# Perceiver layer on one core: the gate-up product kept in PSUM instead of an SBUF tile

## The reference

```
mlp = jax.nn.silu(hidden_states @ Wg + bg) * (hidden_states @ Wu + bu) @ Wd + bd
return mlp + experts_states
```

## Time and profile before

| | |
|---|---|
| median of 3 runs | 934.58 us |
| the profiled execution: its time | 934.41 us |
| the profiled execution: its span | 932.6 us |
| mean granted TensorE clock | 0.969 of full |
| busy: PE, DVE, ACT, POOL | 860.3, 598.5, 467.6, 316.4 us |
| chain that ended last | PE 78%, DVE 11%, ACT 4%, issue 3%, POOL 2%, DMA 1% |

### The profile page before, as it was taken

The page is one execution under the profiler, slowest core; times in us unless marked ns, Lnnn a source line. Parts: engine busy times, 40 slices in busy tenths (PEclk is TensorE's granted clock), DMA queues, the critical chain, the costliest instruction groups (busy, mean ns, idle before and its releaser), DMA issues.

```text
span 932.6 us, 17101 instructions
## 1 busy us (share of the span) xinstructions
PE 860.3 (92%) x6297; PEld 804.8 (86%) x6297; DVE 598.5 (64%) x1542; ACT 467.6 (50%) x1033; POOL 316.4 (34%) x290
## 2 busy tenths in 40 slices
PE   3699999999999999999999999999778777978997
PEld 2599999999999999999999999998567767877885
DVE  6445556556577877555656666776685386765885
ACT  3455554654556564545455555565343254633552
POOL 3544521302021313131220200221692477743442
PEclk9899999999999999999999999999988798989999
DMA  6175332232323232223223233423361042222320
GB/s 195 47 252 159 123 120 91 91 95 91 115 91 129 101 133 92 89 71 123 91 91 118 70 135 113 142 97 100 99 212 60 1 147 91 91 91 81 101 91 24
DMA packets 45219, 99.13 MB, mean 106 GB/s; under 512 B 3744, under 2 KB 16976, under 8 KB 41936
## 3 DMA queue, kind: packets, MB, share of 16 engines
q1 hardware_dynamic: 45040, 98.00, 31.2%
q10 hardware_dynamic: 96, 0.02, 0.0%
HBM read 88.06 MB, written 8.91 MB: 104 GB/s over the span
## 4 chain that ended last, share of the span: by engine, by line
PE 78%; DVE 11%; ACT 4%; issue 3%; POOL 2%; DMA 1%; DVEq 0%; SPq 0%; ACTq 0%
PE pJ L1654 14%; PE pJ L1655 14%; PE pJ L1656 14%; PE pV L1793 7%; PE pS L1771 4%; PE pT L1779 3%; PE pS L1779 3%; PE pT L1771 2%; PE pS L1654 2%; POOL WS L624 2%; PE pS L1656 2%; PE pS L1655 2%; PE pX L1694 1%; DVE KV L1132 1%; DVE late L1611 1%
## 5 line engine op out<-in xcount | busy, mean ns | idle before, releaser
L1654 PE MATMUL pJ<-WV,XT 128*128 128x256 f32 x544 | 159.5, 293 | 0.0
L1655 PE MATMUL pJ<-WV,XT 128*128 128x256 f32 x544 | 154.7, 284 | 0.0
L1656 PE MATMUL pJ<-WV,XT 128*128 128x256 f32 x544 | 154.5, 284 | 0.0
L866 ACT ACTIVATE SP<-SP,xneg 128x768 f32<-128x768 f32 (+1 forms) x96 | 85.8, 895 | 115.4 <-DVE xneg L1239 115.4
L1654 PE MATMUL pJ<-XT,WK 128*128 128x384 f32 (+1 forms) x384 | 126.8, 330 | 4.3 <-POOL XT L657 2.6
L1656 PE MATMUL pJ<-XT,WK 128*128 128x384 f32 (+1 forms) x384 | 125.2, 326 | 0.0
L1655 PE MATMUL pJ<-XT,WK 128*128 128x384 f32 (+1 forms) x384 | 125.1, 326 | 0.0
L1132 DVE TENSOR_TENSOR KT<-pJ,KT 128x384 fp32r<-128x384 f32 x96 | 51.3, 535 | 98.0 <-ACT KT L843 97.9
L657 POOL TENSOR_TENSOR XT<-xtmp,XT 128x384 fp32r<-128x384 f32 (+1 forms) x44 | 41.3, 938 | 196.8 <-ACT XT L827 196.5
L1654 PEld LDWEIGHTS pJ<-WV,XT 128*128 128x128 f32 x544 | 105.1, 193 | 0.2 <-issue 0.2
L1655 PEld LDWEIGHTS pJ<-WV,XT 128*128 128x128 f32 x544 | 105.2, 193 | 0.0
(11 more groups left out here) (362 smaller groups left out, 2177.4 us busy)
## 6 DMA issues: line engine op xcount, KB each, us to landing
WV<-wv_split SPq DMA_DIRECT2D x20, 1024.0 KB, 5.8
WK<-wk_split SPq DMA_DIRECT2D x40, 512.0 KB, 3.6
xraw<-in_ctx SPq DMA_DIRECT2D x7, 768.0 KB, 4.7
wk_split<-WK SPq DMA_DIRECT2D x8, 512.0 KB, 3.7
wv_split<-WV SPq DMA_DIRECT2D x4, 1024.0 KB, 6.5
work<-in_L_ffn_Wd SPq DMA_DIRECT2D x4, 1024.0 KB, 5.2
raw<-in_L_ffn_down_embed SPq DMA_DIRECT2D x8, 512.0 KB, 5.1
work<-in_L_ffn_up_embed SPq DMA_DIRECT2D x4, 1024.0 KB, 5.5
```

The source lines that it names most:

```text
L866: ac.activation(SP[:, I % 2, h, 0:w], SP[:, I % 2, h, 0:w], ACT.Exp, bias=xneg[:, I % 2, h:h + 1], scale=XSC, accum_out=total).then_inc(c_ ...
L1654: te.matmul(dst, a(HI), b(HI), start=start, stop=False)
L1655: te.matmul(dst, a(HI), b(LO), start=False, stop=False)
L1656: return te.matmul(dst, a(LO), b(HI), start=False, stop=stop)
```

## The change

L1587 writes its result back to the PSUM columns from which it reads the up product, instead of to `MA`. L1066 and L1132 read it from there. The bank is thus in use until L1132 is done, so `gate_up` of the tile after next waits for `s_al` in place of `s_a`, and so does the expert transposition `turn(0)`, which writes the first of these banks after tile 15's gates. No instruction is added or removed.

```
@@ -1063,7 +1063,7 @@
                 if ft >= 2:
                     act.wait_ge(s_mo, ft - 1)
-                ac.activation(ACTT[:, ft % 2, HI, :], MA[:, ft % 2, :], ACT.Copy).then_inc(s_ah, 1)
+                ac.activation(ACTT[:, ft % 2, HI, :], pS[:, ft % 2, T2:2 * T2], ACT.Copy).then_inc(s_ah, 1)
@@ -1584,10 +1584,10 @@
                 link(ve.scalar_tensor_tensor(out=MS, in0=pS[:, ft % 2, 0:T2], scalar=1.0, in1=MG[:, ft % 2, :],
                                              op0=ALU.add, op1=ALU.mult))
-                ve.scalar_tensor_tensor(out=MA[:, ft % 2, :], in0=pS[:, ft % 2, T2:2 * T2], scalar=vec[:, Kbu + ft:Kbu + ft + 1],
+                ve.scalar_tensor_tensor(out=pS[:, ft % 2, T2:2 * T2], in0=pS[:, ft % 2, T2:2 * T2], scalar=vec[:, Kbu + ft:Kbu + ft + 1],
                                         in1=MS, op0=ALU.add, op1=ALU.mult).then_inc(s_a, 1)
                 dve.wait_ge(s_ah, ft + 1)
-                low(ACTT[:, ft % 2, LO, :], MA[:, ft % 2, :], ACTT[:, ft % 2, HI, :]).then_inc(s_al, 1)
+                low(ACTT[:, ft % 2, LO, :], pS[:, ft % 2, T2:2 * T2], ACTT[:, ft % 2, HI, :]).then_inc(s_al, 1)
@@ -2016,7 +2016,7 @@
                 if ft >= 2:
-                    pe.wait_ge(s_a, ft - 1)
+                    pe.wait_ge(s_al, ft - 1)
@@ -2062,7 +2062,7 @@
                 else:
-                    pe.wait_ge(s_a, 15)
+                    pe.wait_ge(s_al, 15)
                     turn(0)
```

## The result

The changed kernel takes 926.03 us (median of 4 runs, 925.19 to 926.82) against 934.77 for the kernel before. The ratio is 0.9908, 95% interval 0.989 to 0.9925: 8.7 us faster. That is the forecast direction, but 3 us more than the 5.8 forecast, and inside the range (926.0 to 931.8) by 0.03 us only. The profiled execution took 925.19 us; its span is 923.4, which is 9.2 shorter than before.

A forecast was written before the change was run, and what follows sets the result against it. DVE sets the time in the dense half's front, L1132 running one after the other with POOL. Tile gains sum to 5.5 us, L1066 adds 0.2: 934.4 - 5.7 = 928.7, given as 928.8; range 926.0 to 931.8.

The forecast's parts named there:

- L1132 at 0.42 us with one input in PSUM: DVE's low part in all 16 tiles: 0.42 us instead of 858 ns on average, busy time down 6.9 us.
- Tiles 1 to 3: Gain 1.4 us at tile 1, cut to 1.0 by ACT's queue, then 1.8, 2.8, and 3.7 at the 772.08 matmul.
- POOL's two pieces, tiles 5 and 6: Two of eight POOL pieces PE waits for lose an L1132: 2 x 0.2 = 0.4 us, sum 4.1.
- Tiles 10 and 11: L1561 taken as waiting behind POOL, sum 4.3 us; L1132 of tile 11 adds 0.9, sum 5.2.
- L1587 in PSUM at no cost: L1587 writing to PSUM: 0 us taken, from a span of -0.2 to +2.4 on five of the path's tiles.
- the rival on the slower side: L1587's write into the bank it reads costs far more than a second pass; for instance 938.3 us; chance 0.05.
- L1066: High part copied from PSUM, 383 ns against 0.42 us from SBUF: 0.2 us over six tiles of the path.
- The waits: PE's gate_up and turn(0) wait for s_al, already waited for by the add_tile ahead in its queue: 0.
- The clock: Not counted in the forecast; 1.5 us in one rival, from PE's matmuls at 770 to 775 us at clock 0.50.
- the rival "more": The forecast with 1.2 us for the race and 1.5 for the clock taken off: 926.1 us; chance 0.11.
- Race: L1561 against a POOL piece, tiles 10 and 11, 0.2 us apart: L1561 first keeps 1.4 us, second 0.2; second taken.
- The rival in which the wait only moves on: The next DVE instruction with two SBUF inputs waits for POOL instead of L1132: gain 4.0, 930.6 us; chance 0.22.

The follow-up runs named there:

- taking POOL away: POOL's low-part pieces in the dense half cut from 512 to 8 columns: kernel before 915.5 us (ratio 0.9787), changed kernel 914.3 us (0.9777).
- the small additions: Changed kernel plus an unused 128x4 DVE addition before L1132: both inputs in SBUF 934.26 us (0.9979); one input in PSUM 927.3 us (0.9913).
- The experiment that turned the order round: Changed kernel plus one unused 256-column reduction in front of L1561 of tile 11: 928.09 us (0.994), against 925.77 for the changed kernel beside it.
- the waits alone: Kernel before with only PE's two waits changed from s_a to s_al, product still going to SBUF: 934.62 us (0.9991).

## Why the prediction was right, and where it was short

- *L1132 at 0.42 us with one input in PSUM*: right, 425 ns, in all tiles. That L1132's two SBUF inputs are the cause is shown from two sides, by taking POOL away and by the small additions.
- *Tiles 1 to 3*: forecast 1.4, then 1.8 and 2.8, then 3.7 at PE. Net of the 0.6 head start the trace has 1.4 at L1585 of tile 2 (758.11 to 756.09) and 3.7 at the matmul of 772.08. The step in which ACT's queue limits tile 2 is there too: L1132 starts at 757.81, 0.77 behind the end of L1587. PE's other wait (763.86, for POOL) lay 3.9 us ahead of it and did not count.
- *POOL's two pieces, tiles 5 and 6*: forecast 4.1 in sum, measured 4.1.
- *Tiles 10 and 11*: the first of two terms that were mis-sized. The prediction's own working had L1561 first by 0.2 us (811.9 against 812.1), but it did not trust this and took the lower end, L1561 second, 5.2 in sum at tile 11. L1561 was first, by 0.11 us, and tile 11 has 6.6. The experiment that turned the order round moved tile 11 by 1.4 us.
- *L1587 in PSUM at no cost*: right, 9 ns each; the upper end of 2.4 us and the rival on the slower side are out. *L1066*: 384 ns at the median, as taken. *The waits*: 0, shown alone.
- *The clock*: the second term that was mis-sized. The forecast counted nothing for it; it stood only in the rival "more", with 1.5 us: my estimate from PE's 2.92 us of matmuls from 770 to 775 us at a clock of 0.50, halved. That term also stands behind the range's lower end, 926.0, and no run shows it. The runs show instead that the clock stayed low there for as long: by windows of 1 us it is at 0.50 from 769.4 to 776.2 us before and from 765.1 to 772.0 in the changed kernel, with the first `add_tile(3)` matmul at 0.80 us in both. What a low stretch does to PE can be read in the kernel before: its 128x512 matmuls start 0.43 us apart at 0.50 (L2084 and L2085 at 851.68 and 852.11) and 0.23 apart at 1.00 (856.29 and 856.52). The low stretches are shorter in two other places. Between the first matmuls of `add_tile(11)` and `add_tile(12)`, where the low stretch is half as long (PE had waited 4.61 us in front of it and now waits 2.73), the gain grows by 0.7 us (from 7.25 to 7.93, head start included); around 853 us, where it is gone, by another 0.7 (from 8.5 at 848 us to 9.2 at 857). The trace has 1.7 us behind tile 11 that the forecast lacks, so 0.3 is left over. No run separates the clock from all else.
- *The rest*: 0.6 us before the stage in the profiled execution. It is no part of the change; the other traces of the changed kernel begin the stage at 745.1 and 745.6 us, that with the waits alone at 747.8, the second of the kernel before at 751.8.

Race 1.2, the 1.7 us behind tile 11 and head start 0.6 make the 3.5 us by which the profiled execution undercut the sum. (The last step of that sum, 928.7 and 0.2, is 928.9 and not 928.8; nothing hangs on it.) So the forecast had the mechanism and the size of each step up to tile 10, but the time that came, 926.03, is that of the rival "more" (926.1, chance 0.11), which was the forecast with 1.2 for the race and 1.5 for the clock taken off: the race came true, the clock's low stretches got shorter at other places than the one it named. That 926.03 still lies inside the range is luck. The rival in which the wait only moves on is out: L1556 got shorter, not longer. What did move on is the wait of L1559 in tile 10. Even so L1561 is over 5.7 us earlier there (819.84 to 813.48, less 0.6), near the 5.5 that the working had for L1561 first.

## What to carry to other kernels

When a DVE instruction on the critical path has times that scatter from 0.4 to 1.5 us, look at what POOL does then and count the instruction's SBUF inputs: for the subtraction with two of them, one input in PSUM was enough to take it out of POOL's way, and at 128x256 it cost nothing (425 ns on average instead of 858, and 425 at the median from SBUF with POOL's pieces cut). Look at copies and casts with one SBUF input too; here they waited as well (L1560 1.35 us against 0.28, L1519 1.07 against 0.20). The gain can be larger than the wait that vanishes: here the instruction that no longer queued also spared the next one a POOL piece, in tiles 1, 2 and 10 (in the last two L1556 went from 1.24 us to 0.31 and 0.45). The collision works in both directions (POOL's piece behind L1561 took 3.29 us, alone 1.26): before a long two-input DVE instruction is made earlier, check whether PE waits for what POOL does next, since here L1561, over 4 us earlier, cost some 4 us in the end, more than 2 of them in the dense half.

## What I had not expected of the hardware

An addition of four columns, 0.17 us where POOL was idle (at 825.90), took up to 1.25 us, because it waited for POOL's piece: it ended at 839.82 us, POOL's block at 839.79. L1132 with both inputs in SBUF took up to 1.49 with its 256. And the other way, a POOL piece of 1.26 us took 3.29 when L1561, 2.28 us long, had started 0.11 us before it. With POOL first by 0.19 us it was L1561 that took longer, 3.24 us. In these two traces the engine that was first made the other wait, with 0.1 and 0.2 us between the two outcomes. The low stretches of the granted clock came back in every trace of a kernel (three of the changed one; two of the kernel before and one with the waits alone), so two kernels can differ by a low stretch far behind the place of the edit. What in PE's work decides this no run shows.
